# Cross attention with a two-layer block: key tables fetched through DRAM, query projection in rounded products, and a new order of work

## The reference

```python
x = x + xattn(layernorm(x), ctx, mask, Wq, bq, Wk, bk, Wv, bv, Wo, bo, 16)   # x: (2, 1024, 256), ctx: (2, 77, 256)
x = x + ffn(layernorm(x), router_w, router_b, w1, b1, w2, b2, gamma, beta)

# xattn: 16 heads of 16
q = x @ Wq + bq; k = y @ Wk + bk; v = y @ Wv + bv
att = softmax(scale * q k^T * mask - 1e10 * (1 - mask)); out = (att v) @ Wo + bo
# ffn: the router's weights are replaced by 1 for expert 0, so only w1[0], w2[0] count
h = relu(tgt @ w1[0] + b1[0]); x = tgt + h @ w2[0] + b2[0]
return layernorm(x) * gamma + beta
```

## Time and profile before

| | us |
|---|---|
| median of 3 runs | 211.93 |
| lowest, highest | 211.49, 212.19 |
| the profiled execution, time | 211.63 |
| the profiled execution, span | 209.8 |
| TensorE matmul busy | 195.0 (93%) |
| TensorE weight load busy | 154.2 (74%) |
| VectorE busy | 140.1 (67%) |
| ScalarE busy | 115.9 (55%) |
| GpSimd busy | 89.4 (43%) |
| granted TensorE clock, mean | 0.998 |

### The profile page before, as it was taken

One profiled execution on the slowest core, in us unless ns is written; L12 is line 12 of the kernel. 1 busy time (PEld: TensorE's weight loads), 2 busy tenths in 40 slices (PEclk: granted clock), 3 DMA queues, 4 the chain that ended last, 5 costly groups with the idle time before them and its releaser, 6 DMA issues.

```text
span 209.8 us, 3492 instructions
## 1 busy us (share of the span) xinstructions
PE 195.0 (93%) x1252; PEld 154.2 (74%) x1252; DVE 140.1 (67%) x342; ACT 115.9 (55%) x215; POOL 89.4 (43%) x101
## 2 busy tenths in 40 slices
PE   0499999999899999999999999999999999999990
PEld 0396886645565776779799786878978899988990
DVE  2995869577577987343866673468767377648684
ACT  2377463467789597994222499840548911098100
POOL 7385680028904539232528043711295422901031
PEclk9999999999999999999999999999999999999999
DMA  6998838598553835320200012410001010000212
GB/s 221 392 339 262 287 116 284 189 328 277 167 157 94 276 114 141 130 75 2 75 3 3 0 15 66 127 50 3 0 0 53 0 52 3 0 0 17 77 34 75
DMA packets 14225, 23.62 MB, mean 113 GB/s; under 512 B 1536, under 2 KB 5376, under 8 KB 14208
## 3 DMA queue, kind: packets, MB, share of 16 engines
q1 hardware_dynamic: 13088, 22.08, 32.5%
q10 hardware_dynamic: 1120, 1.32, 1.9%
HBM read 14.35 MB, written 8.39 MB: 108 GB/s over the span
## 4 chain that ended last, share of the span: by engine, by line
PE 83%; DMA 9%; issue 2%; POOL 1%; SPq 1%; DVE 1%; ACTq 1%; POOLq 0%; DVEq 0%
PE W L736 7%; PE W L737 7%; PE W L738 7%; PE W L750 7%; PE W L753 7%; PE W L751 7%; PE T L674 6%; PE acc L686 6%; DMA Sq<-qD 4%; PE M L656 4%; DMA wk<-in_L_xattn_Wk_dram 3%; PE W L695 3%; PE W L589 3%; PE W L590 2%; PE W L582 2%; PE W L713 2%
## 5 line engine op out<-in xcount | busy, mean ns | idle before, releaser
L838 ACT ACTIVATE PT<-T 77x512 f32<-77x512 f32 x64 | 36.0, 591 | 14.9 <-PE T L674 13.6
L750 PE MATMUL W<-w2h,hh 128*128 128x256 f32 x128 | 36.6, 286 | 0.0
L753 PE MATMUL W<-w2h,hl 128*128 128x256 f32 x128 | 36.3, 283 | 0.0
L751 PE MATMUL W<-w2l,hh 128*128 128x256 f32 x128 | 36.1, 282 | 0.0
L975 DVE TENSOR_REDUCE mx<-M 128x6 fp32r<-128x462 f32 (+1 forms) x48 | 26.8, 582 | 10.1 <-PE M L656 9.9
L1162 POOL TENSOR_TENSOR hl<-hr,hh 128x512 fp32r<-128x512 f32 x12 | 16.4, 1371 | 34.8 <-ACT hh L884 34.8
L880 ACT ACTIVATE hr<-W,cst 128x512 f32<-128x512 f32 x32 | 22.0, 686 | 13.3 <-PE W L738 12.0
L736 PE MATMUL W<-x2h,w1h 128*128 128x512 f32 x64 | 25.8, 403 | 0.0
L1040 DVE TENSOR_TENSOR hl<-hr,hh 128x512 fp32r<-128x512 f32 x20 | 14.6, 732 | 16.2 <-ACT hh L884 16.2
L750 PEld LDWEIGHTS W<-w2h,hh 128*128 128x128 f32 x128 | 24.4, 191 | 1.0 <-issue 0.8
L674 PE MATMUL T<-Sq,KS 128*77 128x512 f32 x64 | 24.2, 415 | 1.0 <-DMA Sq<-qD 1.0
(11 more groups left out here) (128 smaller groups left out, 408.2 us busy)
## 6 DMA issues: line engine op xcount, KB each, us to landing
Sq<-qD SPq DMA_DIRECT2D x16, 384.0 KB, 3.7
qD<-qh SPq DMA_DIRECT2D x8, 512.0 KB, 4.2
qD<-ql SPq DMA_DIRECT2D x8, 256.0 KB, 3.1
xin<-in_x_dram SPq DMA_DIRECT2D x3, 512.0 KB, 8.0
out_dram<-xn SPq DMA_DIRECT2D x6, 256.0 KB, 2.1
Mq<-qD SPq DMA_DIRECT2D x6, 192.0 KB, 2.6
w1raw<-in_L_ffn_w_dram SPq DMA_DIRECT2D x2, 512.0 KB, 11.4
w2raw<-in_L_ffn_w_dram SPq DMA_DIRECT2D x2, 512.0 KB, 13.2
```

What stands on the lines that cost most here:

```text
L750: e.matmul(y, hh[:, f, q:q + 128], w2h[:, f * E:(f + 1) * E], start=(f == 0), stop=False)
L751: e.matmul(y, hh[:, f, q:q + 128], w2l[:, f * E:(f + 1) * E], start=False, stop=False)
L753: i = e.matmul(y, hl[:, f, q:q + 128], w2h[:, f * E:(f + 1) * E], start=False, stop=(f == 7))
L838: e.activation(PT[0:TK, m % 6, :], T[m % 2][0:TK, :], ACT.Exp).then_inc(exped, 1)
```

## The change

- The twelve `keys` steps are gone from TensorE, with their copies, `eyer` and the three selection matrices. ScalarE writes the unit rows to both tables (`base`, four copies of 128x1248). SP writes `kh` twice and `kl` once to a new DRAM tensor `kD` (`kout`, three transfers) and reads it to the rows of `KM` (`kload` 0 to 5, three for each half of the heads) and of `KS` (6 and 7).
- The last column of the normalised x is the negative sum of the others, so the projection is written with `Wq[e] - Wq[255]` for the first 255 rows. Row 255 then takes the bias, and the last column of xn the flag of the mask. GpSimd subtracts (`wqd`, with a new transfer `wqb`). The bias product of line 593 is gone.
- For chunks 1 to 3 the projection is done in three rounded products for each half of the 256 rows (`wqh`, `wql`, `xnTh`, `xnTl`); VectorE makes `xnTl` (a new step `turn`) and `wql`, ScalarE `wqh`. Chunk 0 stays with plain float32.
- TensorE gets three idle products (`idle`) of plain float32, 512 columns, from `xin` to `T[0]`, which nothing reads.
- `mT` moves from VectorE to ScalarE. The loads of `wo`, `b2`, `beta` and `gamma` move to much later places on SP. All rows of `TIMES` are new.

```diff
 TIMES = { "PE": {
-        "keys": "11.6 12.5 13.4 17.2 17.7 18.1 20.4 21.1 23.8 24.5 28.9 34.8",
+        "idle": "8.4 18.4 22.3",
...
     "SP": {
-        "late": "0.7 6.1 23.7 62.2",
+        "late": "50.1 68.5 69.9 74.8",
+        "kout": "14.5 17.2 25.2",
+        "kload": "19.2 19.7 20.2 22.2 23.1 24.1 28.4 33.4",
...
+                elif kind == "kout":
+                    i, = a
+                    if i < 2:
+                        fresh.wait_ge(k_high, i + 1)
+                        e.dma_start(kD[i, :, 0:2, :], kh[:, i, :, :].bitcast(F32).rearrange("p b t -> p (b t)")
+                                    .unsqueeze(1).to_broadcast([P, 2, 2 * KP])).then_inc(kh_out[i], 16)
+                    else:
+                        fresh.wait_ge(k_split, 2)
+                        e.dma_start(kD[:, :, 2, :].rearrange("g p n -> p g n"),
+                                    kl[:, :, :, :].bitcast(F32).rearrange("p g b t -> p g (b t)")).then_inc(kl_out, 16)
+                elif kind == "kload":
+                    i, = a
+                    g, r = (i // 3, i % 3) if i < 6 else (i - 6, None)
+                    fresh.wait_ge(kh_out[g], 16)
+                    heads = kD[g].rearrange("(h d) r n -> h d r n", d=D)
+                    if i < 6:
+                        fresh.wait_ge(km_base, g + 1)
+                        e.dma_start(KMg[Q0 + 16 * r:Q0 + 16 * r + 16, g, r::3, :],
+                                    heads[r::3, :, 0, :].rearrange("h d n -> d h n")).then_inc(km_ld[g], 16)
+                    else:
+                        fresh.wait_ge(kl_out, 16)
+                        fresh.wait_ge(ks_base, g + 1)
+                        e.dma_start(KSg[Q0:Q1, g, :, :], heads.rearrange("h d r n -> (d r) h n")).then_inc(ks_ld[g], 16)
...
+                if kind == "idle":
+                    fresh.wait_ge(ld_x0[0], 16)
+                    e.matmul(T[0][:, :], xin[:, 0, 0:128], xin[:, 0:2, :].rearrange("p n e -> p (n e)"),
+                             start=True, stop=True)
...
                 elif kind == "qproj":
                     c, g = a
-                    fresh.wait_ge(xnT_made, 2 * nth["turn", c])
-                    fresh.wait_ge(ld_wq, 16)
+                    fresh.wait_ge(xh_made, 2 * nth["turn", c])
+                    if c in SPLIT_Q:
+                        fresh.wait_ge(xl_made, 2 * SPLIT_Q.index(c) + 2)
+                        fresh.wait_ge(wq_low, 1)
+                    else:
+                        fresh.wait_ge(wq_diff, 2)
                     t = take(step)
-                    e.matmul(t[:, :], wq[:, 0, g * 128:(g + 1) * 128], xnT[:, c % 2, 0, :], start=True, stop=False)
-                    e.matmul(t[:, :], wq[:, 1, g * 128:(g + 1) * 128], xnT[:, c % 2, 1, :], start=False, stop=False)
-                    fresh.wait_ge(bqr_made, 1)
-                    fresh.wait_ge(mT_made, half(c) + 1)
-                    e.matmul(t[:, :], bqr[:, g, :], mT[half(c)][:, :], start=False, stop=True).then_inc(q_made, 1)
+                    for k in range(2):
+                        if c not in SPLIT_Q:
+                            i = e.matmul(t[:, :], wq[:, k, g * 128:(g + 1) * 128], xnTf[:, c % 2, k, :],
+                                         start=(k == 0), stop=(k == 1))
+                            continue
+                        e.matmul(t[:, :], wqh[:, k, g * 128:(g + 1) * 128], xnTh[:, c % 2, k, :], start=(k == 0), stop=False)
+                        e.matmul(t[:, :], wqh[:, k, g * 128:(g + 1) * 128], xnTl[:, c % 2, k, :], start=False, stop=False)
+                        i = e.matmul(t[:, :], wql[:, k, g * 128:(g + 1) * 128], xnTh[:, c % 2, k, :],
+                                     start=False, stop=(k == 1))
+                    i.then_inc(q_made, 1)
...
+                elif kind == "base":
+                    to, g = a
+                    fresh.wait_ge(ld_c, 16)
+                    table, signal = (KM, km_base) if to == "KM" else (KS, ks_base)
+                    e.copy(table[:, 8 * g:8 * g + 8, :, :], eye.unsqueeze(1).unsqueeze(1).to_broadcast([P, 8, 2, KP])
+                           ).then_inc(signal, 1)
...
+                if kind == "wqd":
+                    fresh.wait_ge(ld_wq, 16)
+                    fresh.wait_ge(ld_wqb, 16)
+                    e.tensor_tensor(wq[:, 0, :], wq[:, 0, :], wqb[:, :], ALU.subtract).then_inc(wq_diff, 1)
+                    e.tensor_tensor(wq[0:P - 1, 1, :], wq[0:P - 1, 1, :], wqb[0:P - 1, :], ALU.subtract).then_inc(wq_diff, 1)
```

206 lines of the change are left out of this document (93 added, 113 removed), and 175 rows, old and new, of the table TIMES.

## The result

| | before | after |
|---|---|---|
| median of the runs, us | 211.93 | 209.01 |
| lowest, highest | 211.49, 212.19 | 208.28, 210.63 |
| ratio, 95% interval | | 0.9886 (0.9847 to 0.9924) |
| profiled execution: time, span | 211.63, 209.8 | 208.77, 206.9 |
| TensorE matmul busy | 195.0 | 188.0 |

I forecast 204.5 (202.3 to 207.5). The direction was right, but the gain is 2.9 us instead of 7.4, and the time lies above the range.

A forecast was written before the change was run, and what follows sets the result against it. The prediction took TensorE's queue to bound the kernel. Start of scores -0.6, removed work -7.0 and new waits +0.5 summed to -7.1 us, from 211.63 to 204.5, range 202.3 to 207.5.

The forecast's parts named there:

- What bounds the kernel: Whole span: TensorE's queue bounds, 83% of the span; a wait in the first 60 us is not caught up later.
- part 3: New waits, mainly 24 to 60 us, from fuller VectorE and DMA engines: +0.5 us, bounds -1.0 to +2.5.
- Part 1: Behind the first scores: TensorE's work falls 7.0 us, from key steps 2.8, a turn 0.8, query projections 3.4.
- Part 2: Start of scores: 24.2 us instead of 24.79, a move of -0.6, between -1.8 and +1.4.
- The fixed 2.0 us that I weighed: Key transfers before scores: a DMA's fixed cost by the Trainium skill; by it the sum would be 1.2 lower.
- The sign I had set for being wrong: Scores starting past 27, TensorE resting over 3.5 us between them and 80 us, or projections staying at 2.0.
- Rival 2: Between 24 and 60 us, VectorE's maxima or Sq reads hold TensorE 2.5 us more: 207.5 us; chance 0.13.
- Rival 3: Ahead of scores, TensorE stops for KM and resumes at the lower clock, costing 2.6 us: 207.1; chance 0.04.
- Rival 1: Full yield: scores start at 23.0 and old waits go, giving 202.3 us; chance 0.15.
- rival 4: Keys' path through DRAM so late that scores start beyond 31.8: slower, 212.1 us; chance 0.03.
- Rival 5: Query projections: six rounded products take as long as the old ones, 3.4 us come back: 207.9; chance 0.02.

The follow-up runs named there:

- a_unsplit: Kernel after with the query projections of all chunks in plain float32 instead of rounded products: 210.25 us, ratio 0.9922 to the kernel before.
- d_fill: Kernel after with four more idle products on TensorE between 28 and 36 us: 211.30 us, ratio 0.9953 to the kernel before.
- d_light: Kernel after without any key transfers and with Sq's loads after the first two bringing half their heads: 206.74 us, ratio 0.9759 to the kernel before.
- d_again: Kernel after, unchanged, measured again in a later set: 210.11 us, ratio 0.9898 to the kernel before.
- a_noidle: Kernel after without its three idle products: 211.66 us, ratio 0.9996 to the kernel before.
- a_noks: Kernel after without the two transfers from kD to KS: 209.56 us, ratio 0.9877 to the kernel before.
- a_nokeys: Kernel after without any transfer of the keys, to or from kD: 209.14 us, ratio 0.9878 to the kernel before.
- c_idle4: Kernel after with a fourth idle product right ahead of the first exponential score: 209.98 us, ratio 0.9870 to the kernel before.
- b_mxtwice: Kernel after with four more VectorE reductions between the first and third group of chunk 0's maxima: 211.27 us, ratio 0.9960 to the kernel before.

## Why the prediction was wrong, by its own steps

- **What bounds the kernel: read wrongly.** "Almost every microsecond of TensorE's queue is a microsecond of the end" held behind 80 us, and a busy TensorE ahead of it was taken as the bound. But it was busy because projections in plain float32 and key steps stood between chain steps. Taken off there, they left waits: TensorE rests 2.28 us where it rested 0, and a_unsplit and d_fill give 0.8 us for 2.0 and 1.2 for 3.4 of work (1.4 and 2.3 in the profiled executions). This is the step that failed; with the +0.5 of part 3, which follows from it, it carries nearly the whole miss. That waits arose is shown; that each microsecond of them is cover lost is argued from these two runs and from what is left over in d_light.
- **Part 1, right as a size.** 7.0 forecast, 6.9 measured; six products 1.39 for 1.44.
- **Part 2, right in the total (24.2 against 24.46), by luck: its terms were off in both directions.** The weights came later (20.07 instead of 18.2), kD took 6.4 instead of 4.2, landing at 20.86 and not 18.8; the KM reads took 2.0 to 2.6 instead of 3.7, and the last landed at 24.31, where I had 24.3. TensorE, which I had at 23.0, reached the scores no sooner: 0.70 for `wqd`, because `wqb` landed only at 12.70, and 1.22 for `ql`, none of it in my sum. The DMA view of 10 to 25 us has a 7 and an 8 among its nines and a 4 in slice 25, which I passed over; it changes little. The fixed 2.0 us that I weighed lie near the six KM reads (1.95 to 2.58) and far from the writes (6.4 and 5.7). The Trainium skill, DMA: Bandwidth & Descriptors, section "Anatomy of one DMA", gives them for DMAs on GpSimd's path, and these were issued by SP.
- **Part 3, the failed term.** +0.5 forecast, +4.4 found (as what is left of 6.9 behind a gain of 2.5). I took the value nearer to the lower end "because TensorE has projections of three chunks to put between"; those are the very projections that had just been made shorter by 0.6 us each. I wrote that TensorE's share of the stretch shrinks by some 6 us, and drew from it only that VectorE would be fuller, not that what it had hidden would come out. The upper end, 2.5, was too low too. VectorE did not go near full (11.84 of 15.21); it stands in the chain all the same, between the scores and the maxima's transfer (28.96 to 30.5 us above).
- **The sign I had set for being wrong** appeared: TensorE rests 2.28 + 0.58 + 1.39 = 4.25 us between the scores and 80 us, more than 3.5.
- **Rival 2** had the right place, 24 to 60 us, and the right kinds of waits, at 2.7 instead of 4.4; its chance of 0.13 was too low. My argument against it, that TensorE had no rest before beside such a VectorE, was the misreading again.
- **Rival 3** is real in single executions (d_again) and in kernels with a little more wait (a_noidle), but the profiled execution of the kernel after shows no fall between 13 and 204 us, so it does not explain its 208.77. It widens the spread, and it blurs the prices of several experiments. My argument against it, that 1.11 us of rest had brought no fall, did not carry over: its 0.04 was too low for a kernel that rests more.
- **Rivals 1, 4 and 5** did not happen. The sum of rival 4 names two hops at 5.6 us but holds only the second (11.2); with both, its start of the scores would be later than 31.8.

The sum with the terms found: -0.33 - 6.9 + 4.4 = -2.8, to 211.63 gives 208.8, against 208.77. It must close, since 4.4 is itself a difference; it shows sizes, not the cause.

Open: what the keys' path is worth by itself. No run had the keys on TensorE in the new order. Nor did any run shorten VectorE's reductions. No kernel that computes the whole beats the kernel after by more than the measurement can tell.

## What to carry to other kernels

A fully busy engine need not be the bound: ask what the removed work was covering. Follow the chain of the stage (here scores, reductions, transposed maxima, transfer, exponential) with the filler taken out, and if its length is near that of the stretch, price removed work at a fraction. Idle products put into the suspected stretch measure that fraction cheaply: here 3.4 us of them cost 1.2. In known waits they give its lower end. Look at the granted clock of each execution before you take a price from it.

Taking one transfer out of a loaded set moves the wait to the next one (a_noks, a_nokeys). Count bytes and issues apart: 18% fewer bytes with 18 more issues was slower, for whichever of the reasons above.

## What the hardware showed that I had not expected

- A VectorE instruction of 405 ns took 1369 beside a GpSimd subtraction of 1.35 us and 691 beside a cast of 0.68.
- A transfer of 8 KB took 1.8 us at a quiet moment and 3.9 to 5.3 behind others, with no gain from the other issuing queue (4.85 and 4.39); a write of 156 KB took 6.4 beside the weights and 3.3 without w2's.
- When the first 8 KB were issued counted for little: in eight profiled executions with the same transfers ahead of them they were issued between 30.68 (c_idle4) and 32.43 us (b_mxtwice) and landed between 34.96 and 35.92.
- The clock fell 0.1 to 2.4 us after single rests of 0.69 to 2.03 us, in some executions of a kernel and not in others: after 1.29 ahead of 35.97 in the kernel after it did not.
